# An audio tower on one core: the token weights' four transfers issued from ScalarE's queue

## The reference

```
h = layer_norm(x, g1, b1)                       # 448 x 1024
h = layer_norm(h @ W + b, g2, b2)               # W: 1024 x 512
h = h + attention(norm(h), W_Q, W_K, W_V, W_O)  # 16 heads of 128, causal over the 7 patches
x_q = fp8_e4m3(norm(h) / scale)                 # scale = max|norm(h)| / 448
h = h + x_q @ (weight * weight_scale).T + bias  # 512 x 512
```

## Time and profile before

| | |
|---|---|
| timed runs | 277.38, 276.91, 275.63 us; median 276.91 |
| the profiled execution, first to last instruction | 274.0 us |
| TensorE matmul busy | 265.6 us, 97% |
| VectorE busy | 155.7 us, 57% |
| ScalarE busy | 128.6 us, 47% |
| DMA | 23.82 MB, mean 87 GB/s |
| mean granted TensorE clock | 0.994 |

### The profile page before, as it was taken

How to read it: one execution, slowest core, us unless ns; L and a number is a source line. 1 busy time by engine, 2 the same in 40 slices (tenths; PEclk the granted TensorE clock), 3 DMA queues, 4 the chain that set the end, 5 groups by cost and what they waited for, 6 DMA issues and landing times.

```text
span 274.0 us, 3908 instructions
## 1 busy us (share of the span) xinstructions
PE 265.6 (97%) x1484; PEld 222.3 (81%) x1484; DVE 155.7 (57%) x323; ACT 128.6 (47%) x218; POOL 0.2 (0%) x4
## 2 busy tenths in 40 slices
PE   7899998999999999999999999999999999999995
PEld 6344445999889898989898998989898989888963
DVE  4469978655555445362645554453626455478892
ACT  2653952454435344435444353444354443365460
POOL 0000000000000000000000000000000000000000
PEclk9799999999999999999999999999999999999999
DMA  6999000134214030404132130404030300000004
GB/s 181 324 261 404 18 0 1 28 128 153 80 75 151 2 153 0 153 0 153 19 134 69 84 144 10 153 0 153 0 153 19 134 0 0 0 4 0 0 2 134
DMA packets 5444, 23.82 MB, mean 87 GB/s; under 512 B 1019, under 2 KB 1483, under 8 KB 3260
## 3 DMA queue, kind: packets, MB, share of 16 engines
q1 hardware_dynamic: 5436, 23.71, 25.4%
HBM read 22.79 MB, written 0.92 MB: 87 GB/s over the span
## 4 chain that ended last, share of the span: by engine, by line
PE 92%; DVE 3%; DMA 2%; SPq 1%; ACT 1%; issue 1%; DVEq 0%
PE bank L269 15%; PE bank L271 14%; PE bank L270 14%; PE acc L304 11%; PE acc L392 9%; PE bank L368 5%; PE acc L396 5%; PE bank L376 5%; PE bank L382 2%; PE acc L498 2%; PE bank L361 2%; PE bank L277 2%; DMA tokw_raw<-tok_w 2%; PE acc L453 1%; PE acc L468 1%; SPq L223 1%
## 5 line engine op out<-in xcount | busy, mean ns | idle before, releaser
L269 PE MATMUL bank<-ht_hi,qkvw_hi 128*128 128x448 f32 (+2 forms) x204 | 74.4, 365 | 0.9 <-DVE ht_lo L721 0.9
L271 PE MATMUL bank<-ht_hi,qkvw_lo 128*128 128x448 f32 (+2 forms) x204 | 72.9, 357 | 0.0
L270 PE MATMUL bank<-ht_lo,qkvw_hi 128*128 128x448 f32 (+2 forms) x204 | 72.8, 357 | 0.0
L721 DVE TENSOR_TENSOR qkvw_lo<-raw,qkvw_hi 128x1536 fp32r<-128x1536 f32 x16 | 28.1, 1757 | 34.0 <-ACT qkvw_hi L520 34.0
L269 PEld LDWEIGHTS bank<-ht_hi,qkvw_hi 128*128 128x128 f32 x204 | 38.4, 188 | 4.1 <-issue 1.0
L270 PEld LDWEIGHTS bank<-ht_lo,qkvw_hi 128*128 128x128 f32 x204 | 38.4, 188 | 2.8
L271 PEld LDWEIGHTS bank<-ht_hi,qkvw_lo 128*128 128x128 f32 x204 | 38.4, 188 | 2.7
L721 DVE TENSOR_TENSOR z_lo<-bank,z_hi 128x448 fp32r<-128x448 f32 x15 | 9.4, 624 | 42.2 <-ACT z_hi L520 42.2
L304 PE MATMUL acc<-tokw_raw,xt 128*112 128x512 f32 x64 | 30.5, 621 | 1.1 <-DMA tokw_raw<-tok_w 1.1
L520 ACT CAST qkvw_hi<-raw 128x1536 fp32r<-128x1536 f32 x16 | 23.6, 1485 | 0.0
L304 PEld LDWEIGHTS acc<-tokw_raw,xt 128*112 128x112 f32 x64 | 11.2, 186 | 14.8 <-issue 10.4
(11 more groups left out here) (115 smaller groups left out, 347.3 us busy)
## 6 DMA issues: line engine op xcount, KB each, us to landing
raw<-heads_w SPq DMA_DIRECT2D x16, 1024.0 KB, 4.9
tokw_raw<-tok_w SPq DMA_DIRECT2D x4, 512.0 KB, 7.2
x_in<-patches SPq DMA_DIRECT2D x3, 448.0 KB, 9.3
ffnw_raw<-ffn_w SPq DMA_DIRECT2D x1, 1024.0 KB, 19.2
out<-h_sb SPq DMA_DIRECT2D x3, 224.0 KB, 2.3
x_in<-patches SPq DMA_DIRECT2D x2, 224.0 KB, 2.8
g_row<-tok_g SPq DMA_DIRECT2D x1, 224.0 KB, 11.3
b_row<-tok_b SPq DMA_DIRECT2D x1, 224.0 KB, 12.2
```

The source lines that it names most:

```text
L269: nc.tensor.matmul(ps, hi, whi, start=first, stop=False, skip_group_check=True)
L270: nc.tensor.matmul(ps, hi, wlo, start=False, stop=False, skip_group_check=True)
L271: return nc.tensor.matmul(ps, lo, whi, start=False, stop=last, skip_group_check=True)
L721: return nc.vector.tensor_tensor(dst, src, hi.bitcast(F32), ALU.subtract)
```

## The change

The four transfers of the token weights are no longer issued by the sync engine, where they stood behind tile 1 (three of them) and tile 2 (the fourth). ScalarE issues all four as the first thing in its program. Sizes, destinations and semaphores stay.

```diff
@@ block.sync @@
-            def load_tokw(i):
-                a, b = TOKW_PIECES[i]
-                load(tokw_raw[:, a:b, :], tok_w[:, a:b, :], tokw_landed[i])
-
             load(b1_col[:], tok_b1, cols_landed)
             load(x_in[:, 1, :], patches[1], x_landed[1])
-            load_tokw(0)
-            load_tokw(1)
-            load_tokw(2)
             load(x_in[:, 2, :], patches[2], x_landed[2])
-            load_tokw(3)
             load(tok_b_raw[:], tok_b, tok_b_landed)
@@ block.scalar @@
         def _(act):
+            for i, (a, b) in enumerate(TOKW_PIECES):
+                act.dma_start(tokw_raw[:, a:b, :], tok_w[:, a:b, :]).then_inc(tokw_landed[i], 16)
+
             def hi_part(dst, src):
```

## The result

The changed kernel takes 280.67 us (median of four runs, 280.44 to 280.82), the kernel before 276.27 beside it; the ratio is 1.0186, with a 95% interval of 1.0148 to 1.0223. So it is slower by 4.4 us, clear of the 1% that I had set as what can be told, where I had forecast +1.7 and no change beyond 1%. The ratio is that of the fast runs as recorded; the quotient of the two medians is 1.016. The kernel before was timed again beside the experiments, with medians of 275.5, 274.91 and 275.5 us; the changed one was not, and against these medians its loss would be 5.2 to 5.8 us. A timed run is about 1.8 us longer than its span (280.72 and 278.9), so differences of spans and of times can be compared. The time lies inside the range (275.7 to 281.3), in the part that belonged to the second rival, to which I had given 0.28.

What follows compares the result with a forecast made beforehand. TensorE, busy for 97% of the span, was taken as the bound, so its delayed start moves the end: tile 1's transposes at 15.85 instead of 14.10, later waits 0, giving 276.91 + 1.7 = 278.6 us; range 275.7 to 281.3.

Steps and rivals of the forecast that it cites:

- the second rival: Start of kernel: weights served before tile 0, or TensorE's clock falls again; clearly slower, middle 280.2 us, chance 0.28.
- Issues: Sync queue and ScalarE: later sync issues 1.4 to 1.9 us earlier, buying little; ScalarE's four issues hidden, cost 0.
- Tile 0 by turns, +1.9: Tile 0's landing: packets taken in turn with the weights delay it 1.9 us; first embedding near 10.1.
- Tile 1, +2.75: Tile 1's landing: 1.5 MB of new weights ahead, less free DMA time, delay it 2.75 us to 10.85.
- The first four chunks "end before 15.85 either way": TensorE's first embedding: from 10.1, fast or slow, ends at 13.5 or 15.1, before tile 1's transposes at 15.85.
- The fixed 4.88 behind the landing: VectorE and ScalarE: tile 1 takes a fixed 4.88 us from landing to normalised, ready at 15.73.
- no later wait that takes the delay up: After tile 1's transposes: tile 2 and bias waits are covered, cost 0, so the delay reaches the end.
- The rule that only issue time is saved: DMA queues: several issuing engines share 16 DMA engines, saving only issue time; alone, sum 0, time 276.9 us.

Runs made afterwards that it cites:

- the order on one queue: Kernel before, all transfers on the sync queue but the weight pieces interleaved with tile 0 and the small loads, ahead of tile 1; 281.02 us, ratio 1.0177.
- The run with the clock kept up: Changed kernel with 34 in place of 14 matmuls of ones ahead of the first transposes; 281.56 us, ratio 1.0211.
- one piece: Changed kernel with only the first weight piece issued by ScalarE, the other three back on the sync queue; 278.19 us, a single run.
- tile 1 first: Changed kernel with tile 1 issued ahead of the identity and the two columns on the sync queue; 282.47 us, ratio 1.0231.
- two pieces: Changed kernel with only the first two weight pieces issued by ScalarE, the other two back on the sync queue; 279.63 us, ratio 1.0134.
- the small loads on ScalarE: Kernel before with the identity and the two columns issued by ScalarE at its start, the weights staying on sync; 277.31 us, ratio 1.0099.

## Why the prediction was wrong

- **Issues.** Right. Four issues of 2.22 us in all on ScalarE, hidden; the first wait for the weights gone; the sync queue's later issues 1 to 1.4 us earlier, where 1.4 to 1.9 were expected (tile 2 in the second half of 3.36 to 4.66 in place of 4.96, the bias row at 4.70 in place of 6.07) and worth nothing.
- **Tile 0 by turns, +1.9.** Right in kind, too small: +2.87 and +3.73. The rows-in-turn sum of 2.2 us, shortened by free time, took the best rate of the trace. In fact the engines moved 141 GB/s between 2 and 3 us at a share of 0.78, where tile 0 alone had moved 320 before. The kernel before has the same mark where its own 4 KB rows begin (136 GB/s at 0.84 between 4 and 5 us); I had read it as free time. Whether it is the length of the rows that makes this start slow is not shown: with the weights in rows of 2 KB the rate was still 197 and 201 GB/s between 2 and 4 us.
- **Tile 1, +2.75. This is the step that failed.** It landed 5.87 later. I had counted 0.6 MB of the weights, moved before 8.1 us, as ahead of tile 1 already, and so only 1.5 MB as new. But they stood behind tile 1 in the same queue and merely overlapped with its landing: tile 1's last row starts at 5.90 and VectorE starts on the tile at 8.10, and in between 0.64 MB of what stands behind it go. In the changed kernel these times are 11.72 and 13.97, and 0.60 MB of what stands behind it go in between. By the time VectorE starts on tile 1, 1.68 MB had been moved before and 3.74 MB now, 2.06 more. All 2.10 MB are new: 2.10 MB / 357 GB/s = 5.9 us. And I had taken off 1.45 us of free DMA time, of which only 0.09 MB came back, 0.3 us. With both corrected my own sum gives 5.6, against 5.87 measured; the order on one queue, tile 1 at 14.10, shows that these bytes carry the delay. That 5.8 was my upper bound is luck, since it came from other numbers (1.5 MB at 259 GB/s).
- **The first four chunks "end before 15.85 either way".** Wrong, and not noticed as a chain of its own: tile 0's +3.73, the unpriced wait for the column (1.23), the slow transposes (1.73 for 0.96) and 5.85 us of slow chunks bring TensorE to 18.73. It happens to tie with tile 1. The second rival came near the time (280.2 against 280.67) by luck: tile 0 was not 5.0 us late, and the four chunks after tile 1's transposes ran fast (3.44 us from 19.91), so neither of its two ways is what happened. The run with the clock kept up shows that the clock by itself adds nothing to this kernel's time.
- **The fixed 4.88 behind the landing, no later wait that takes the delay up, all of it reaching the end.** Right: 4.89; 4.82 at the transposes, 4.85 at the last bias, 4.9 in the span. Had the 5.87 stood in the sum in place of 2.75, it would have read 13.97 + 4.88 + 0.12 - 14.10 = +4.87.
- **The rule that only issue time is saved.** On bandwidth the traces agree with what the Trainium skill ("DMA: Bandwidth & Descriptors", Issuing engines are not separate DMA queues) says: 350 GB/s between 8 and 12 us, 357 before. It is half of the story: which queue a transfer stands in also sets what stands ahead of the others, here by 5.87 us for tile 1.

## What to carry to other kernels

A transfer moved to a second queue is not only sooner itself: everything in the first queue now shares with it. In these traces it shares row by row, so small loads and short rows lose most beside long ones. Before such a move write down, for each landing that someone waits for, all bytes that will be taken before it in the new order, and take nothing off for bytes that merely overlapped in the old trace or for a DMA share below 1. And look for a second chain that ends just behind the first: here one piece and tile 1 first brought tile 1 in sooner, and then tile 0 or the small loads, with the slow chunks behind them, held the stage.

## What I had not expected of the hardware

- A 4 KB load (the b1 column, 128 rows of 32 bytes) landed about 9 us after its issue at 2.82 beside 4 KB rows on the other queue; before, it took 3.1.
- The sync engine's issues became slower while the weights were in front: 0.66 us for the g1 column in place of 0.43. This is no matter of the second queue: with all on one queue the third piece's issue took 0.91 us, in place of about 0.46.
- The granted clock in the windows reads 1.00 at the start, and matmul times say otherwise: 28 records of ones take 5.57 us (0.20 each) at the start of the changed kernel, where 10 take 1.15 later, and with two pieces and with the small loads on ScalarE the transposes took 1.73 us under a clock shown as 1.00. When the low level ends differs from run to run of near-equal starts (embedding from 9.14: 4.96 us before, 4.48 with the small loads moved), which may be part of the scatter of 275.55 to 278.59 us in that last kernel.
